# Self-attention in a perceiver block: value product with swapped operands, quarters taken by POOL, one output product for four

## The reference

```python
qkv = x @ W_qkv + b_qkv
q, k, v = jnp.split(qkv, 3, axis=2)      # 16 heads of 8
energy = jnp.einsum('bqhe,bkhe->bqhk', q, k)
attn = jax.nn.softmax(energy, axis=-1) / sqrt(E)
out = jnp.einsum('bihv,bvhd->bihd', attn, v)
out = out.reshape(B, N, E)
return out @ W_out + b_out
```

## Time and profile before

| | us |
|---|---|
| median of 3 runs | 1492.02 (1490.94 to 1494.69) |
| profiled execution | 1491.5, of it the span of the instructions 1489.3 |
| busy in the span | PE 1326.8 (89%), PEld 1010.5, DVE 1217.0 (82%), ACT 1101.6 (74%), POOL 702.9 (47%) |
| mean granted clock of PE | 0.957 of 2.4 GHz |
| self-attention stage, 504 to 637 us | PE busy 128.44, DVE 103.44, ACT 69.58, POOL 41.33 |

### The profile page before, as it was taken

One profiled execution on the slowest core, in us unless ns is written; L12 is line 12 of the kernel. 1 busy time (PEld: TensorE's weight loads), 2 busy tenths in 40 slices (PEclk: granted clock), 3 DMA queues, 4 the chain that ended last, 5 costly groups with the idle time before them and its releaser, 6 DMA issues.

```text
span 1489.3 us, 46126 instructions
## 1 busy us (share of the span) xinstructions
PE 1326.8 (89%) x15863; PEld 1010.5 (68%) x15863; DVE 1217.0 (82%) x3478; ACT 1101.6 (74%) x1844; POOL 702.9 (47%) x464
## 2 busy tenths in 40 slices
PE   5898999999978699969887898999999999898988
PEld 3676777777857599936665666766676666666666
DVE  6799999998997788778788777787877878787885
ACT  2698999999978255538777677777787778677776
POOL 7276777777768433223332233443444344333323
PEclk9999999999987599979999899999999999999999
DMA  5975766666642478400000000000000000000000
GB/s 154 233 194 158 190 178 185 187 172 188 180 135 65 122 195 198 112 1 2 2 0 0 0 1 2 0 0 0 0 0 0 0 0 0 2 7 14 7 14 15
DMA packets 196200, 108.46 MB, mean 73 GB/s; under 512 B 89740, under 2 KB 194028, under 8 KB 196076
## 3 DMA queue, kind: packets, MB, share of 16 engines
q1 hardware_dynamic: 122032, 84.65, 20.4%
q10 hardware_dynamic: 74044, 22.17, 6.8%
HBM read 67.62 MB, written 39.03 MB: 72 GB/s over the span
## 4 chain that ended last, share of the span: by engine, by line
DVE 20%; PE 14%; issue 13%; ACT 5%; DVEq 2%; ACTq 0%
PE pair L1734 7%; PE pair L1716 5%; DVE hs L1647 4%; ACT gf L1589 3%; ACT gh L1594 2%; DVE xc L1621 2%; DVE gl L1633 1%; DVE rs L50 1%; DVE rs L52 1%; DVE st L1612 1%; PE pair L1746 1%; DVE rs L48 1%; DVE rs L37 1%; DVE mv L1616 1%; DVE sel L1699 1%
## 5 line engine op out<-in xcount | busy, mean ns | idle before, releaser
L1576 POOL TENSOR_TENSOR gl<-gf,gh 128x1024 f16<-128x1024 f32 x128 | 292.6, 2286 | 543.9 <-ACT gh L1594 543.9
L1589 ACT ACTIVATE gf<-pair,b1c 128x512 f32<-128x512 f32 x512 | 326.6, 679 | 149.1 <-PE pair L1716 148.9
L1734 PE MATMUL pair<-w2p,gh 128*128 (+1 forms) x4096 | 366.9, 222 | 12.0 <-DVE gl L1633 12.0
L1734 PE MATMUL pair<-w2p,gl 128*128 (+1 forms) x2048 | 358.1, 222 | 0.0
L1734 PEld LDWEIGHTS pair<-w2p,gh 128*128 128x128 f16 x4096 | 326.5, 99 | 37.7 <-issue 8.4
L407 POOL TENSOR_TENSOR pl<-p,ph 128x1024 f16<-128x1024 f32 x128 | 272.7, 2131 | 125.5 <-ACT ph L464 125.2
L1716 PE MATMUL pair<-xh,w1p 128*128 128x512 f16 x1024 | 327.1, 381 | 3.6 <-DVE w2p L1363 2.9
L1594 ACT ACTIVATE gh<-gf 128x1024 f16<-128x1024 f32 x256 | 270.6, 1057 | 25.2 <-ACT gf L1589 2.0
L1633 DVE TENSOR_TENSOR gl<-gf,gh 128x1024 f16<-128x1024 f32 x128 | 169.0, 1320 | 122.7 <-ACT gh L1594 120.6
L1734 PEld LDWEIGHTS pair<-w2p,gl 128*128 128x128 f16 x2048 | 203.5, 99 | 0.0
L1716 PE MATMUL pair<-xl,w1p 128*128 128x512 f16 x512 | 195.0, 381 | 0.0
(11 more groups left out here) (232 smaller groups left out, 2518.8 us busy)
## 6 DMA issues: line engine op xcount, KB each, us to landing
KS<-k_parts_dram SPq DMA_DIRECT2D x64, 384.0 KB, 4.5
k_parts_dram<-kh SPq DMA_DIRECT2D x64, 256.0 KB, 3.3
cx<-in_ctx_dram ACTq DMA_DIRECT2D x30, 512.0 KB, 4.4
k_parts_dram<-kl SPq DMA_DIRECT2D x64, 128.0 KB, 3.5
w1p<-in_L_ffn_w_dram SPq DMA_DIRECT2D x8, 512.0 KB, 6.1
w2p<-in_L_ffn_w_dram SPq DMA_DIRECT2D x8, 512.0 KB, 8.0
QS<-q_parts_dram ACTq DMA_DIRECT2D x128, 24.0 KB
Q<-q_parts_dram SPq DMA_DIRECT2D x32, 96.0 KB
```

The source lines that it names most:

```text
L1576: pool.tensor_tensor(gl[u.m2][:, 0:h, :], gf[u.m2][:, 0:h, :], gh[u.m2][:, 0:h, :], ALU.subtract).then_inc(d_loP, 1)
L1589: act.activation(gf[u.m2][:, c, :], hb[c][:, :], ACT.Gelu, scale=1.0 / WS, bias=b1c[:, u.step.expert(u.e), c]).then_inc(d_g, 1)
L1734: last = pe.matmul(yb[v.m2][:, t * D:(t + 1) * D], g[:, c, t * P:(t + 1) * P], w2p[:, le, part, c, :].rearrange("p a h -> p (a h)"), start ...
```

## The change

- The value product has pT as its weights and V2 moving, so it gives rows (h, q) and columns (b, g, h', d). Only the diagonal part h = h' is wanted.
- ACT evicts all of it to `of`. POOL takes the diagonal in four instructions, one for each 32 rows, and multiplies by the reciprocals in the same instruction, into `on2` (128 x 128). The multiplication of the 128x512 probabilities goes.
- DVE transposes `on2` in 32x32 blocks to `oT2`, rows (h, g, d) and columns (b, q), and the output product is one matmul with `Wout`, whose rows are loaded in the order of the heads (h, g, d). `WoutM`, `rowsel` and `sel3` go.
- The layer norm of xm goes from DVE to ACT as scale and bias (`nb2` is minus mean times the inverse deviation), in slot 3 ahead of that slot's evictions. The first block keeps the form on DVE.
- The scaling of `Wout`, the copy of the value bias and their product move into the cross-attention stage.

```diff
@@ sync, cross-attention stage, s == 2
-                        sp.dma_start(Wout[:, :], W_out).then_inc(c_w, 16)
+                        for j in range(GH):
+                            sp.dma_start(Wout[GD * j:GD * (j + 1), :],
+                                         W_out.rearrange("(g j d) n -> j g d n", j=GH, d=DH)[j]).then_inc(c_w, 16)
+                            sp.dma_start(bv2_c[GD * j:GD * (j + 1), :],
+                                         b_qkv[2 * D:3 * D].rearrange("(g j d a) -> j g d a", j=GH, d=DH, a=1)[j]).then_inc(c_w, 16)
@@ scalar, cross-attention stage
+                    if s == FIRST - 4:
+                        act.wait_ge(c_w, CW)
+                        act.activation(Wout[:, :], Wout[:, :], ACT.Copy, scale=float(D) ** -0.5).then_inc(c_wm, 1)
+                        act.activation(bv2R[:, :], bv2_c[:, 0:1].broadcast_to((P, D)), ACT.Copy).then_inc(c_wm, 1)
@@ gpsimd
-                            if nm is not None:
-                                i = (w + 1) % 4
-                                pool.wait_ge(c_rc, nm + 1)
-                                pool.tensor_tensor(pr[i][:, :, :, :], pr[i][:, :, :, :],
-                                                   rc2[i][:, :, :].unsqueeze(3).broadcast_to((P, PB, G, SQ)),
-                                                   ALU.mult).then_inc(c_nrm, 1)
+                            if pv is not None:
+                                i, r = (w + 1) % 2, (w - 1) % 4
+                                pool.wait_ge(c_rc, pv + 1)
+                                pool.wait_ge(c_oc, pv + 1)
+                                pool.wait_ge(c_bias, f.n + 1 if f else NBLK)
+                                wait(pool, c_oT, pv - 1)
+                                for h in range(GH):
+                                    own = slice(SQ * h, SQ * (h + 1))
+                                    pool.tensor_tensor(on2[i][own, :, :, :], of[i][own, :, :, h, :],
+                                                       rc2[r][own, :, :].unsqueeze(3).broadcast_to((SQ, PB, G, DH)),
+                                                       ALU.mult).then_inc(c_on, 1)
@@ scalar
+                            if w == 3 and st.block(3):
+                                b = st.block(3)
...
+                                for k in range(4):
+                                    t = bass.ds(4 * b.n + k, 1)
+                                    act.activation(xm[:, k, :], xs[:, t, :].rearrange("p a c -> p (a c)"), ACT.Identity,
+                                                   scale=rs2[:, t], bias=nb2[:, t]).then_inc(c_xm, 1)
...
-                                wait(act, c_y, pv - 1)
-                                act.activation(oT2[i][:, :, :, :].rearrange("p h b q -> p b h q"),
-                                               bank[6][:, :].rearrange("p (b h q) -> p b h q", b=PB, h=GH),
+                                wait(act, c_on, GH * (pv - 1))
+                                act.activation(of[i][:, :, :, :, :].rearrange("p b g h d -> p (b g h d)"), bank[6][:, :],
                                                ACT.Copy).then_inc(c_oc, 1)
@@ vector
-                            if w == 3 and st.block(3):
-                                normalise(st.block(3))
...
+                                wait(dve, c_on, GH * (nm - 3))
...
+                            if pv is not None:
+                                i = (w + 1) % 2
+                                dve.wait_ge(c_on, GH * (pv + 1))
+                                wait(dve, c_y, pv - 1)
+                                dve.transpose(out=oT2[i][:, :, :].rearrange("p b q -> p (b q)"),
+                                              in_=on2[i][:, :, :, :].rearrange("p b g d -> p (b g d)")).then_inc(c_oT, 1)
@@ tensor
-                                pe.wait_ge(c_nrm, tr + 1)
+                                pe.wait_ge(c_exp, tr + 1)
...
                                     last = pe.matmul(bank[6][:, b * P:(b + 1) * P],
+                                                     pT[(w + 1) % 2][:, b * P:(b + 1) * P],
                                                      V2[m][:, t * PB + b, :, :].rearrange("k g c -> k (g c)"),
-                                                     pT[(w + 1) % 2][:, b * P:(b + 1) * P], start=True, stop=True)
+                                                     start=True, stop=True)
...
-                                pe.wait_ge(c_oc, y + 1)
+                                pe.wait_ge(c_oT, y + 1)
                                 wait(pe, c_yr, y)
-                                for h in range(GH):
-                                    last = pe.matmul(bank[7][:, 0:D], oT2[w % 2][:, h, :, :].rearrange("p b q -> p (b q)"),
-                                                     WoutM[:, h, :], start=(h == 0), stop=(h == GH - 1))
-                                last.then_inc(c_y, 1)
+                                pe.matmul(bank[7][:, 0:D], oT2[w % 2][:, :, :].rearrange("p b q -> p (b q)"), Wout[:, :],
+                                          start=True, stop=True).then_inc(c_y, 1)
```

84 lines of the change are left out of this document (37 added, 47 removed).

## The result

The changed kernel takes 1513.34 us (median of 4 runs, 1511.12 to 1514.34) against 1492.42 for the kernel before, measured with it (4 runs, 1490.94 to 1494.69). The ratio is 1.0137 [1.0119, 1.0154]. It is slower by 20.9 us. The forecast was 1498.0, and the time lies above its range. The profiled execution has a span of 1512.5 us against 1489.3, so 23.2 of difference are there to be placed.

The account below looks back on a forecast made before the run. PE was taken to set the pace in self-attention. From 1491.5 us, +8.0 for that stage (+7.5 steps, +0.5 tail and drain) and -1.6 for the start gave 1497.9, so 1498; range 1485 to 1507, the forecast's own 1493 to 1502.

Parts of the forecast that it names:

- The rest: Permuted loads, a few ACT, PE and DVE operations in cross-attention, three POOL operations less: costed at nothing.
- The new wait: Self-attention: loop over two slots through POOL, transpose and DVE to PE's scores; step 17.7 against 16.25 us, +7.5 over five.
- The clock falls: Rival: in self-attention PE's gaps lower the granted clock, +10 over 5.5 steps, 1508; chance 0.06.
- POOL's burst: Self-attention: POOL's four 32x128 products per tile take 3 x 0.40 + 0.43 = 1.6 us in a row.
- the transpose: DVE's 128x128 block transpose per self-attention tile: 0.30 us, 0.22 until the next instruction starts.
- the normalisations: Four per self-attention step move from DVE to ACT, ahead of two evictions: 0.39 us each, 1.56 per step.
- the rival with the short burst: Self-attention: POOL's four operations overlap, 0.43 + 3 x 0.1 = 0.7 us; step 15.9, total 1485; chance 0.20.
- Tail and drain: End of self-attention: last eight tiles +1.6, against savings in the drain of the last three; together +0.5 us.
- The start: Start of self-attention: four products that build WoutM go, so PE's projection comes sooner; -1.6 us, ends 0 and 3.0.

Follow-up runs that it names:

- e1: The changed kernel with POOL's three small selector operations put back between two set-up fills, result unused; 1501.48 us.
- e2: The kernel before with POOL's three selector operations moved behind the fills of Q and V; 1497.37 us.
- e5: The kernel before with 43 short ACT instructions added in the set-up between self-attention and the expert stage; 1504.09 us.
- e6: The changed kernel with 85 more short ACT instructions at that set-up place, 128 in all; 1501.17 us.

## Why the prediction was wrong

The direction was right, the size was not. It forecast +6.4 in the profile's own time (8.0 - 1.6), and the trace has +23.2. That the direction came out was luck: the self-attention stage, in which the forecast put the loss, is 1.6 shorter in this trace. By its steps:

- **The rest, "I cost them at nothing".** This step failed, twice. "Three POOL operations less there" was read as work taken away. They were the gap in which DVE's copies got in, worth 6.1 to 6.8 us at the end of cross-attention (e1, e2). And the ACT operations were counted by their busy time, while 43 instructions in front of the expert loop went with 18.6 there (18.4 in the profile of e5, which has nothing else). The expert stage was in no term and in no rival, although it is more than half the span, and although its DVE and POOL met within 0.1 us in the trace of before.
- **The new wait, loop of 17.7.** That there is a loop through POOL and the transpose was right: the transpose waited for POOL for 1.2 us or more in two slots of four. How it closes was wrong. In the step of e6 without a fall of the clock it takes 16.4, of which the pair with a query or key projection is 8.24 (forecast 8.2) and the pair with the value projection 8.18 (forecast 9.5). PE's scores don't wait for the differences in it. With the value projection the loop closes through the output product, which PE has in front of the next scores and which waits for the addition into xs (1.26 there). That is the shorter way round. With the query or key projection it goes on through maxima and differences, but then through DVE's low halves L1248 to PE's next projection, which waits 0.92 for them. The sum left the low halves out and put the scores in, so that 8.24 met 8.2 is in part luck. PE was busy for 14.21 of 16.40 us, 87%, not 77%; in the stretch of the earlier trace rows of the kernel after it is 92%.
- **The clock falls.** It had been a rival at 0.06, and it came beside the loop, not instead of it: granted 0.90 over the stage, 0.6 us a step. Loop and clock gave +3.3 over five steps, where +7.5 was forecast.
- **POOL's burst, the transpose, the normalisations.** 1.82 against 1.6, because the pitch is 0.475 and not the 0.40 of the row it was taken from; 0.31 against 0.30; 1.54 against 1.56. The quarters ran one behind the other, as the two fills had suggested, and the rival with the short burst fell. The 0.1 in its sum had no row behind it; 0.475 was measured.
- **Tail and drain.** +0.5 forecast, -1.2 in this trace. Five others with the same code have -0.8 to +1.9, so the sign isn't settled. Not followed up.
- **The start.** -1.6 was taken from bounds of 0 and 3.0. It gave -3.7, and -3.1 to -4.8 in the other profiles, more than the upper bound: the slot with the WoutM products went from 6.70 to 3.70, and 0.7 more came back around it.

Open: why ACT's passage from step to step takes 0.08 us more or less with the place of its code (43 against 64 and 128 instructions); and why the clock fell in some self-attention steps and not in others. PE's wait was 1.18 us ahead of a fall, and 1.26 in e6's step without one.

## What to carry to other kernels

Ask of every operation that is removed what got in beside it, and of every instruction that is added ahead of a loop what comes out of step behind it, also in stages whose code is not touched. Where DVE and POOL operations that hold each other up start within 0.1 us of one another in the trace, give the order a wait of its own: here one line was worth 14 us in the kernel before. Compare a changed kernel with its partner at the same place of the code, or the accident is taken for the change.

## What the hardware showed that was not expected

- POOL's fills drew two DVE copies out to 7.4 us, over the two boundaries of three back-to-back fills. In e2 they ended at 34.2, at the boundary of the second and the third.
- A POOL operation of 2.12 us held a 128x128 DVE operation for 1.9 us (0.34 to 2.24), and even one of 128x4 (0.16 to 2.04). When DVE came first, POOL's took 3.36 instead of 2.14, and the step stayed at 23.9.
- With POOL's second operation 5.17 to 5.19 us behind its first, which of the two engines came first was open: DVE lost 35 times and won seven. At the 5.27 and 5.28 of the steady steps it always won.
- 43 idle instructions in the set-up of ACT made the kernel before 12.5 us slower (1504.09 against 1491.61, measured together). 64 made it 6.2 faster (1485.29 against 1491.53).
- Four POOL products on four different quarters of the partitions took 0.40 each, one every 0.475, and 1.82 together: they didn't overlap.
